# Gated cross-attention and a top-1 mixture of eight experts: nested surplus bodies, down weights first, and x of batches 2 to 7 behind the first context half

## What is computed

```python
# x (8, 256, 256); ctx (8, 120, 256); H = 256; experts E = 8 with I = 704
x = x + tanh(g_xattn) * attention(layernorm(x), ctx)     # Q, K, V with biases, softmax / 16
h = layernorm(x)                                         # 2048 tokens
e = argmax(h @ router_w.T)                               # one expert per token
for each expert e:                                       # for its own tokens alone
    y = (silu(h @ gate_w[e].T) * (h @ up_w[e].T)) @ down_w[e].T
x = x + tanh(g_ffn) * y
```

## Time and profile before

| | us |
|---|---|
| median of 3 runs | 230.23 (230.07 to 230.31) |
| the profiled execution | 230.14 |
| its span | 228.3 |
| TensorE busy | 184.3 (81%) |
| VectorE (DVE) busy | 109.3 (48%) |
| ScalarE (ACT) busy | 109.8 (48%) |
| GpSimd (POOL) busy | 135.2 (59%) |

### The profile page before, as it was taken

The page is one execution under the profiler, slowest core; times in us unless marked ns, Lnnn a source line. Parts: engine busy times, 40 slices in busy tenths (PEclk is TensorE's granted clock), DMA queues, the critical chain, the costliest instruction groups (busy, mean ns, idle before and its releaser), DMA issues.

```text
span 228.3 us, 4589 instructions
## 1 busy us (share of the span) xinstructions
PE 184.3 (81%) x1367; PEld 167.8 (74%) x1367; DVE 109.3 (48%) x366; ACT 109.8 (48%) x251; POOL 135.2 (59%) x143
## 2 busy tenths in 40 slices
PE   7799999997686499979929989966998999996000
PEld 3466899885586299968929988966996999995000
DVE  2488799966597136333305437224355345362000
ACT  2267787765320567856246766527776053140000
POOL 3002269597473897389889479979869940401100
PEclk9999999999587789999997999997999999999555
DMA  6999213947700209321931920691021010100100
GB/s 189 337 388 375 105 48 87 354 137 236 250 0 24 86 4 355 110 84 27 351 114 34 362 90 19 254 355 45 3 59 40 1 50 6 48 4 4 49 9 3
DMA packets 11722, 29.11 MB, mean 127 GB/s; under 512 B 1928, under 2 KB 8537, under 8 KB 10646
## 3 DMA queue, kind: packets, MB, share of 16 engines
q1 hardware_dynamic: 6320, 20.20, 24.9%
q0 software_dynamic: 1920, 4.53, 6.2%
q10 hardware_dynamic: 3430, 3.74, 4.9%
HBM read 24.26 MB, written 4.52 MB: 126 GB/s over the span
## 4 chain that ended last, share of the span: by engine, by line
PE 52%; issue 10%; DMA 10%; POOL 9%; DVE 4%; ACT 4%; ACTq 1%; SPq 1%; POOLq 1%; DVEq 0%
PE ps L1100 19%; PE ps L1132 12%; DMA both<-in_WdL 7%; POOL wgu L490 6%; DMA both<-in_ctxT 4%; PE ps L964 3%; PE ps L903 3%; PE ps L985 3%; PE ps L944 3%; PE ps L933 3%; POOL xin L541 2%; PE ps L974 2%; PE ps L924 2%; POOL out L550 1%; PE ps L1078 1%
## 5 line engine op out<-in xcount | busy, mean ns | idle before, releaser
L1100 PE MATMUL ps<-xhT,wgu 128*128 128x256 f32 (+2 forms) x528 | 74.5, 301 | 12.5 <-ACT V L781 8.7
L1100 PEld LDWEIGHTS ps<-xhT,wgu 128*128 128x128 f32 x528 | 71.1, 200 | 15.2 <-ACT V L781 9.6
L490 POOL TENSOR_TENSOR wgu<-raw_gu,wgu 128x352 fp32r<-128x352 f32 (+1 forms) x28 | 52.7, 1916 | 8.4 <-ACT wgu L678 8.3
L1132 PE MATMUL ps<-wd,hT 128*128 128x256 f32 (+1 forms) x340 | 41.9, 282 | 0.6 <-issue 0.3
L1132 PEld LDWEIGHTS ps<-wd,hT 128*128 128x128 f32 (+1 forms) x340 | 40.4, 180 | 1.1 <-issue 1.1
L550 POOL DMA_INDIRECT out<-xin,table x20 | 19.7, 985 | 34.5 <-DVE xin L1438 30.6
L1416 DVE TENSOR_TENSOR ps<-V,ps 128x256 f32<-128x256 f32 (+2 forms) x40 | 17.8, 446 | 42.8 <-PE ps L1100 28.1
L499 POOL TENSOR_TENSOR wd<-both,wd 128x512 fp32r<-128x512 f32 (+1 forms) x12 | 28.6, 2394 | 0.0
L781 ACT ACTIVATE V<-ps 128x256 f32<-128x256 f32 (+2 forms) x40 | 15.7, 394 | 20.4 <-PE ps L1100 20.1
L541 POOL DMA_INDIRECT xin<-x_rows,table x20 | 19.4, 971 | 9.9 <-issue 9.9
L678 ACT ACTIVATE wgu<-raw_gu 128x704 fp32r<-128x704 f32 (+2 forms) x34 | 24.0, 773 | 1.6 <-issue 1.5
(11 more groups left out here) (146 smaller groups left out, 240.6 us busy)
## 6 DMA issues: line engine op xcount, KB each, us to landing
raw_gu<-in_Wgu SPq DMA_DIRECT2D x8, 1408.0 KB, 6.5
both<-in_Wd SPq DMA_DIRECT2D x8, 640.0 KB, 5.0
x_rows<-x ACTq DMA_DIRECT2D x8, 256.0 KB, 3.5
xin<-in_x SPq DMA_DIRECT2D x7, 256.0 KB, 10.5
both<-in_WdL SPq DMA_DIRECT2D x16, 64.0 KB, 5.3
both<-in_ctxT ACTq DMA_DIRECT2D x2, 480.0 KB, 9.4
xin<-x_rows,table POOLq DMA_INDIRECT x20, 3.0
out<-xin,table POOLq DMA_INDIRECT x20
```

The lines of the kernel that those rows point to most:

```text
L490: pool.tensor_tensor(lo[where], raw[where], hi[where].bitcast(F32), ALU.subtract)
L1100: last = pe.matmul(ps[:, bank, 0:n], weights(j, w_part, c, i, kind), xhT[:, j % 2, x_part, c, 0:n], start=(c == 0 and (w_part, x_part) == ...
L1132: last = pe.matmul(y_of(k, size), hT[:, h_part, some], wd[:, j % SPLIT, i, w_part, :], start=(s == 0 and n == 0 and k % 2 == 0), stop=(s = ...
```

## The change

- `surplus`: the body of turn k+1 stands inside the `If` of turn k.
- Down weights get their places by `room_d`: experts 0 to 2 place 1, then 0, 1, 0, 1, 0. The load of expert 3 waits for the sort's tables to be read (`t_stat`), and each load of down weights stands ahead of the next expert's gate and up. In the attention loop ACT and POOL split down before gate and up.
- SP waits for the first context half before x of batches 2 to 7. ACT issues that half before x of batch 1.
- The seven unread matmuls are gone.
- POOL: gather and low parts of j+2 stand ahead of the scatter of j-1, and the counts are read behind the first two fetches of each gather.
- ACT: `split_d` in two halves, the second one two chunks later; `turned_x(0)` ahead of the third block; one Silu of a small tile ahead of the wait for the counts; `sent` is gone from here. It stands on SP behind `surplus`, for which SP reads the eight counts, and in POOL's first surplus turn.
- TensorE waits for the third block of tokens (`v_xhT3`) only where it reads it.

```diff
+        def room_d(j):
+
+            return 1 if j < SPLIT else (j + 1) % 2
...
-            for k in range(MORE):
-                with eng.If(n_more > k):
-                    run(E + k)
-                    eng.sem_inc(idle, 1)
+
+            def turn(k):
+                if k < MORE:
+                    with eng.If(n_more > k):
+                        run(E + k)
+                        turn(k + 1)
+                        eng.sem_inc(idle, 1)
+
+            turn(0)
...
             sp.dma_start(wv[:], ap(Wv, C)).then_inc(d_wv, 16)
+            sp.wait_ge(d_ctx[0], 16)
             for b in range(2, B):
...
             def load_d(j, of, tail):
-                if j == SPLIT + 1:
+                if j == SPLIT:
 
                     sp.wait_ge(t_stat, 1)
                 elif j:
 
-                    sp.wait_ge(a_hd, j if j <= SPLIT else j - 1)
-                    sp.wait_ge(p_ld, j if j <= SPLIT else j - 1)
-                place = raw_d[:, 1 if j <= SPLIT else j % 2]
+                    sp.wait_ge(a_hd, j if j < SPLIT else j - 1)
+                    sp.wait_ge(p_ld, j if j < SPLIT else j - 1)
+                place = raw_d[:, room_d(j)]
...
+            load_d(0, Wd[0], WdL[0])
             load_gu(0, Wgu[0])
-            load_d(0, Wd[0], WdL[0])
             load_gu(1, Wgu[1])
-            for e in range(1, E):
-                if e + 1 < E:
-                    load_gu(e + 1, Wgu[e + 1])
+            for e in range(1, SPLIT):
                 load_d(e, Wd[e], WdL[e])
+                load_gu(e + 1, Wgu[e + 1])
+            load_d(SPLIT, Wd[SPLIT], WdL[SPLIT])
+            for e in range(SPLIT + 1, E):
+                load_gu(e, Wgu[e])
+                load_d(e, Wd[e], WdL[e])
+            sp.wait_ge(v_used, 1)
+            sizes = [count(sp, j) for j in range(E)]
...
             surplus(sp, "sp", run)
...
+            for r in (3, 4, 0, 1, 2):
+                sent(r)
...
             for e in range(SPLIT - 1):
+                low_d(e, 3)
                 low_gu(e, 4)
-                low_d(e, 3)
...
             for j in range(E):
-                if j:
-                    scatter(j - 1)
                 if j + AHEAD < E:
                     gather(j + AHEAD)
-                    sizes.append(count(pool, j + AHEAD + 1))
                 if SPLIT <= j + AHEAD < E:
                     low_gu(j + AHEAD, 1)
                     low_d(j + AHEAD, 1)
+                if j:
+                    scatter(j - 1)
...
+            cv = ctxT.rearrange("(c p) n -> p c n", c=C)
+            act.dma_start(ctx_sb[:, :, 0:480], cv[:, :, 0:480]).then_inc(d_ctx[0], 16)
             act.dma_start(xin[:, TB:2 * TB, :], x[1].rearrange("(t p) h -> p t h", p=P)).then_inc(d_x[1], 16)
-            cv = ctxT.rearrange("(c p) n -> p c n", c=C)
-            for n in range(2):
-                act.dma_start(ctx_sb[:, :, 480 * n:480 * n + 480], cv[:, :, 480 * n:480 * n + 480]).then_inc(d_ctx[n], 16)
+            act.dma_start(ctx_sb[:, :, 480:960], cv[:, :, 480:960]).then_inc(d_ctx[1], 16)
...
                 chunks(j, 0, 2, sizes[j])
-                if j and SPLIT <= j + AHEAD < E:
-                    split_d(j + AHEAD)
+                now = j and SPLIT <= j + AHEAD < E
+                if now:
+                    split_d(j + AHEAD, 0)
...
                     gathered3(j + 1, sizes[j + 1])
+                if now:
+                    split_d(j + AHEAD, 1)
                 chunks(j, 4, CI, sizes[j])
...
-            for r in (3, 4, 0, 1, 2):
-                sent(r)
-            act.sem_inc(a_sent, 1)
...
             query_bias()
-            for _ in range(7):
-                pe.matmul(ps[:, 7, 0:2 * H], quiet[:, 0:P], quiet[:], start=True, stop=True)
             score_weights(0)
```

69 lines of the change are left out of this document (41 added, 28 removed).

## The result

The changed kernel took **220.76 us** (median of 4 runs, 217.5 to 225.6) beside 230.27 us before (4 runs), a ratio of 0.9477 [0.9414, 0.954]. Forecast were 206.7 us within 200 to 216, so the sign was right and the time was not. The profiled execution took 219.08 us, its span 217.3. The prediction took the noise to be 0.2% from the kernel before; the changed kernel spread by 3.7%.

What follows compares the result with a forecast made beforehand. Bounds: TensorE's six far-code skips in the tail, ACT's waits for down weights in the experts. From 230.14 us, -11.7 (nesting), -12.0 (experts), +1.5 (head), -1.0 and -0.2 (experts' start) gave 206.7, range 200 to 216.

Steps and rivals of the forecast that it cites:

- Nested bodies, -11.7: Tail: one far-code fetch of 3.16 us replaces six on TensorE; tail 7.6 us in place of 19.26, -11.7 us.
- The short branch: Skill's rule for surplus skips: compare-and-branch about 108 ns, so six cost 0.65 us and nesting would give 0.5.
- Rival B: Tail is not made of skips and stays 19.26 us whatever the number of `If` statements: 218.4 us, chance 0.05.
- Down weights and POOL's order, -12.0: Experts 1 to 7: earlier down weights remove ACT's two DMA waits; 104.3 us against 116.35, -12.0 us.
- What would be left without any stall, 98.1: Experts 1 to 7: floor of 98.1 us if nothing stalls, against 116.35 measured.
- I leave 2.0, 1.2, 0.8, 1.2 and 1.0 us: Experts 1 to 5: time left above the floor because ACT still splits weights there, giving 104.3 in all.
- Start of the experts, -1.2: Before expert 0: first gather not waiting for the count read, -1.0; TensorE not waiting for the empty third block, -0.2.
- The head, +1.5: Before the loop: swapping context and x of batch 1 delays the norm chain and first transpose, +1.5 us.
- rival D: Attention loop runs at 1.2 GHz after longer idle: up to 32.6 us more, 239, slower than before; chance 0.03.
- the unread matmuls alone do nothing: Head: the seven unread matmuls stand in the wait for the context, so removing them changes nothing.
- rival A: Experts: stalls get a new owner, ACT, and only 8.5 us of DMA waits go: 210.2 us, chance 0.2.
- the new order of splits in the loop: Front: down split before gate and up keeps POOL busy some 3 us longer before the sort, where it idled: 0.

Runs made afterwards that it cites:

- d3_late: The changed kernel with expert 3's down weights loaded only after the gathers of experts 0 and 1: 216.51 us on chip 11, 217.12 us on chip 10.
- scatter_first: The changed kernel with POOL's old order in the experts, scatter of j-1 ahead of gather and low parts of j+2: 225.12 us on chip 10.
- after_4: The changed kernel, unchanged, run again as control on chip 10: 221.85 us.
- after_unnested: The changed kernel with the six surplus `If` statements side by side again: 232.94 us on chip 11.
- fill: The changed kernel with only the seven unread matmuls put back ahead of the score weights: 207.69 us on chip 5.
- before_again: The kernel before, unchanged, run again for a trace on chip 4: 228.71 us.
- after_third: The changed kernel, unchanged, run again as control on chip 4: 206.85 us.
- late_head: The changed kernel with the whole old head back and expert 3's down weights loaded behind the second gather: 201.05, 201.36 and 216.19 us on chips 5, 4, 10.

## Why the prediction was wrong, step by step

*Nested bodies, -11.7.* **Right.** The tail fell by 11.96 us to 7.30 (7.6 forecast), POOL's drain ends it, TensorE drains 2.7 us behind its last matmul. Alone it took 10.1 and 10.4 us off the tail in the traces. The short branch of the Trainium skill's Advanced Engine Details and Errata, Control Flow Timing (0.65 us for six, an estimate from its figure) is contradicted by the nested kernel alone, and the measurement decides. Rival B is out: it had 218.4 us, and the 218.3 to 220.8 that came lie near it by chance alone, since the tail that it kept is gone.

*Down weights and POOL's order, -12.0.* **The mechanism was right, and the term mis-sized by 4.25 us** in the profiled pair: experts 1 to 7 fell by 7.75, to 108.6 and not 104.3. None of the sixteen traces of changed kernels, on any chip, has a wait of ACT for the down weights; the four of the kernel before and its nested form have two or three each, the one in the earlier trace rows that names no releaser counted. "What would be left without any stall, 98.1" was right to 0.3 on chip 5. What failed is the sentence "I leave 2.0, 1.2, 0.8, 1.2 and 1.0 us", 6.2 us for ACT's splits: they cost 0.3 us on chip 5, and the 10.5 left here are waits of another kind, which the earlier trace rows had shown in expert 1 (18.02 us without a wait for a DMA) and which I had read as ACT's load. What these waits are waits for stays open.

*Expert 0.* **A missing term of +5.47.** I left it at 13.88 because no step of the change touches it. It took 19.35 us here and 18.83 on chip 10, and 14.15 and 14.29 in d3_late and scatter_first, which change nothing in it; on chips 5 and 4 it took 14.47 and 14.56. So it is of the same kind as the waits above.

*Start of the experts, -1.2.* **Wrong in sign: +2.15.** The first gather came 0.94 us sooner behind the table, as taken. But I listed that expert 3's load now waits for the sort, and asked only when it would be early enough, not what it would lie beside: it starts 1.1 us behind the first gather and slows it. The later load takes back 2.4 to 2.7 us. It's the one miss that could have been foreseen from the trace before: there the loads of down weights took a median 5.0 us to land, and the earlier trace rows had the gather's place.

*The head, +1.5.* **Right in mechanism, 0.91 in the profiled pair, 2.0 over all traces.** The first transpose stands at 12.50 to 16.47 us in the eight traces with the old head (median 13.1), and at 14.77 to 15.64 in eleven with the new one (median 15.1). Beside it stands the clock, which I had kept out of the sum: in 5 to 26 us no trace with the old head has a low stretch, and nine of the eleven with the new head have one (3.4 to 6.7 us at 1.2 GHz, from the mean grant of the stretch). It isn't what makes the first transpose late, since the two traces without a low stretch have it at 14.77 and 15.13. It costs time where it falls into the loop: from the first transpose to the start of the last batch's the fifteen traces with a grant of 1.00 take 29.7 to 30.2 us, three with 0.95 take 31.1 to 31.3, and two with 0.90 (after_4 and after_unnested) 33.0. So rival D was right in kind, and small: 1.3 to 3.3 us in five of the twelve traces with the new order of loads (fill is the twelfth), nothing in the loop of the others, the first trace among them. That the unread matmuls alone do nothing was right (fill).

*Sum of the misses:* 4.25 + 5.47 + 3.35 - 0.41 - 0.26 = 12.40 us, the distance from 206.7 to 219.1. My range ended at 216 since rival A had only 3.5 us for stalls that get a new owner; they were 9.7 with expert 0.

*That 206.3 and 206.9 came out on chips 5 and 4 doesn't make the working right.* On chip 4 the pair before_again and after_third fell by 18.0 us of span: tail -11.4, experts 1 to 7 -13.5, expert 0 +0.6, and the start of expert 0 +6.3 (from 78.49 to 84.77) where I had +0.3. Of these 6.3 the head is 2.1 and the gathers' stretch 2.1; the other 2.1 lie between first transpose and table. The changed kernels take 55.5 to 60.9 us there, the kernel before and its nested form 55.4 to 56.8. On chip 4, 1.4 of the 2.1 are the low clock in the loop that the head brought. The end of the loop, from the last batch's transpose to the first matmul of the sort, adds 2.1 (19.2 in place of 17.1), and the sort gives 1.4 back. That end takes 17.1 to 18.1 us in the four traces of the kernel before and its nested form, at a mean grant of 0.90 to 0.96, and 17.4 to 21.8 in the sixteen changed ones, at 0.73 to 0.94. The four of these with the old head (19.1 to 21.5) show that it isn't the head's. TensorE's longest wait there, for ACT's `pT`, is 0.9 to 1.4 us in the four and 1.2 to 2.9 in the sixteen. I had put the new order of splits in the loop at 0, and ACT does them there; but no run undoes it alone, so that this is the cause isn't shown.

The fastest kernel that holds for any counts is late_head: 201.05 and 201.36 us on chips 5 and 4, 216.19 on chip 10, 5 to 7 us under the changed kernel each time. On chip 10 the later load alone does as well.

## What to carry to other kernels

Several `If` statements that are false together, with bodies of far code, are worth nesting: here one skip cost TensorE some 3 us at the end of the program, with the rest of the change and without it. When a load is released earlier, ask beside what it will run: here it fell on the first gathers and cost more than the earlier gather gave. And when a long wait is taken away, what it covered decides the gain: here the changed kernel showed 15 us between chips, where the old one had shown 6. So time such a change on more than one chip.

## What the runs showed of the hardware

- One program, with the same 23 and 25 instruction packets, takes 206.2 and 206.9 us on two chips, 221.9 on a third and 218.3 where it was first timed (217.5 to 225.6 over all runs there); the kernel before takes 225.4 and 226.6 on the first two and 229.8 to 231.3 elsewhere.
- A false `If` over the body of one surplus turn costs TensorE 3.0 to 3.5 us (six instruction packets of 16 KB at this distance in the tail before).
- Of the waits behind this, that in expert 3 keeps its place: expert 3 takes 20.97, 21.05, 20.75 and 21.01 us in four traces of the changed kernel and d3_late on such chips, and 16.56 on chip 5. An edit in expert 3's load takes 4.4 to 5.2 us off expert 0 and puts 1.6 to 1.9 on expert 1.
- 768 KB of weights beside an indirect gather: the first block is there 4.81 us after its issue in place of 3.29.
- TensorE's clock after the idle times in the head (1.86 us ahead of the score weights and 0.99 behind them in the first trace, 2.98 behind them in fill): 3.4 to 6.7 us at 1.2 GHz in most traces, now in the score weights, now in the loop, where it cost 1.3 to 3.3 us. A page of the Trainium skill that bears on this, TensorE: Matmul & The Clock Gate, Part 1, has activity lift the clock; the traces agree, since no loop stayed low: the grant is back at 1.00 by 26 us in all of them.
